# A graph-attention kernel: the fold of W1 as columns over two pairs of banks, and x, score rows, W1 and mask stores in other places

## The chip, the cores and the metric

The kernel runs on one core of a Trainium2 chip. The metric is device time in microseconds, of which a lower one is better, as the median of several executions. The core has five engines with a queue of instructions each: TensorE (PE), VectorE (DVE), ScalarE (ACT), GpSimd (POOL) and SyncE (SP); SyncE issues all transfers here.

## The reference

Two graph-attention layers over the same edges, with a residual and a layer norm.

```python
x, src, dst = ...                       # (1250, 768), 20000 edges, sorted by dst
src = concatenate([src, arange(1250)]); dst = concatenate([dst, arange(1250)])

def _gat_layer(x, src, dst, W, a_src, a_dst, bias, concat):
    h = (x @ W).reshape(N, H, C)
    al_s = einsum('nhc,hc->nh', h, a_src)
    al_d = einsum('nhc,hc->nh', h, a_dst)
    e = leaky_relu(al_s[src] + al_d[dst], 0.2)
    m = segment_max(e, dst)
    ex = exp(e - m[dst])
    alpha = ex / (segment_sum(ex, dst)[dst] + 1e-16)
    out = segment_sum(h[src] * alpha[:, :, None], dst)
    out = out.reshape(N, H * C) if concat else out.mean(axis=1)
    return out + bias

h   = elu(_gat_layer(x, src, dst, W1, att_src1, att_dst1, b1, concat=True))   # W1 768 x 2048, 4 heads of 512
out = _gat_layer(h, src, dst, W2, att_src2, att_dst2, b2, concat=False)       # W2 2048 x 768, 1 head
result = layernorm(x + out)
```

## The kernel before

Nodes are cut into ten blocks of 125 (B = 125, NB = 10). The edges become a dense count matrix C, and each layer is then a dense attention over blocks. The change touches only the first part of the program, up to the first attention chunk.

**Windows.** C is built in NW = 30 windows of 41 or 42 destination columns. For each window w VectorE makes seven one-hots (L1338, `ring`) from a table that ScalarE shifted (L987), TensorE multiplies them onto the slots' one-hots (`oh_lo`, L1714) between an opening product with zeros (L1706) and a closing one (L1717), and ScalarE copies the result into C (L993, "strip"). Window w uses bank w % 3 and waits until the window before the last but one has been copied. The `for w in range(NW)` loops of PE, ACT and DVE carry all other work of this part between windows, each at window numbers given by the constants XW, FS, CT, WSPL and WROW.

**The fold.** The attention vectors are multiplied into W1, so that the scores come straight from x. For each of 16 blocks of 128 columns of W1 (`fold_step`, L1637): six transposes of 128x128 into banks 3 and 4 (L1645), a copy to `wT` by ScalarE (L1018), and a product with the 8 columns of `acz` as weights and wT's 768 columns moving, into 8 rows of banks 5 and 7 (L1655). FS = 8 steps go ahead of window 0, two follow it, and one each window 1 to 7. Then ScalarE copies the 8x768 rows to `warow` (L1023, L1024), TensorE transposes them back to columns (L1766), and they are rounded to `wahi` and the rest `walo` (fp32r pairs: every exact product is three: hi x hi, hi x lo, lo x hi, L1683 to L1685).

**x.** From window XW - 1 = 10 on one block of x a window is transposed (L1674) in banks 6 and 7; ScalarE rounds it to the high part of `xa` (L963, L964), VectorE subtracts for the low part (L1308, L1310). SyncE stores both parts of each block to `xT_scratch` (L656), for heads 1 to 3. The raw x (`xall`) lies where W1's three tiles will be, so W1 can be loaded only when all of x has been transposed.

**Counts and masks.** From window CT = 8 on, every third window, the counts of one block are clipped (L1326), transposed into banks 3 to 5 (L1726), turned into a mask by ScalarE (L1001, L1003; two buffers, so mask b waits for the store of mask b - 2), stored by SyncE (L650), and later loaded back (L671) for the maxima on VectorE (L1364).

**Score rows** (L1738) are computed in windows 21, 22 and 23, a group of blocks each, when all of x is ready, into banks 6 and 7.

**W1 of head 0** is loaded (L644) behind the store of the tenth block, rounded by ScalarE after windows 26 to 28 (L968) and its rest made by GpSimd (L897). Then TensorE makes h in ten blocks (L1696), eight of them before the shift `gcol` is needed.

[...]

## Time and profile before

| | us |
|---|---|
| runs (three) | 952.14, 952.80, 955.18 |
| median | 952.8 |
| the profiled execution | 957.13 |
| its span, first to last instruction | 955.3 |
| TensorE busy | 887.2 (93%) |
| VectorE busy | 606.9 (64%) |
| ScalarE busy | 424.1 (44%) |
| GpSimd busy | 223.3 (23%) |
| mean granted TensorE clock | 0.977 |

The trace is one execution. Busy time is that of each engine's own instructions; a line L is one of the kernel before. TensorE's weight loads (PEld) run beside its products. A granted clock of 1.00 is full speed, 0.50 half.

### The profile page before, as it was taken

The numbers are of one execution on the slowest core, as the hardware profiler recorded it, in microseconds if no ns is written. First come the engines' busy times: TensorE is split into PE (matmuls) and PEld (weight loads), VectorE is DVE, ScalarE is ACT, GpSimd is POOL, SyncE is SP. The second block draws the span as 40 slices with busy tenths as digits, with TensorE's granted clock in tenths as the row PEclk, the third lists the DMA queues.
The fourth block names the chain that finished last, engine by engine and source line by source line (L and its number), as shares of the span: only waits on it lengthen the run. The fifth ranks groups of instructions, "written<-read, shape, count | busy, mean of one in ns | idle before, by whom it ended". The sixth has DMA issues, their size and how long they took to land.

```text
span 955.3 us, 15152 instructions
## 1 busy us (share of the span) xinstructions
PE 887.2 (93%) x5719; PEld 800.6 (84%) x5719; DVE 606.9 (64%) x1155; ACT 424.1 (44%) x686; POOL 223.3 (23%) x148
## 2 busy tenths in 40 slices
PE   4997885999999999999999998989999999699996
PEld 2455553889888998889988897989999999699996
DVE  9547743658893698828887388663222344397887
ACT  5346433257643675437663385852111111387300
POOL 1000003035321243122431266500000000154452
PEclk9999897999999999999999999999999999889999
DMA  8508994553467334582164333446232441400223
GB/s 299 134 1 119 151 169 134 137 151 132 158 193 189 121 115 139 170 202 95 38 193 117 103 132 121 135 142 150 54 84 47 78 75 30 98 3 2 59 88 97
DMA packets 64451, 111.19 MB, mean 116 GB/s; under 512 B 31772, under 2 KB 33464, under 8 KB 63004
## 3 DMA queue, kind: packets, MB, share of 16 engines
q1 hardware_dynamic: 64379, 110.22, 45.1%
q8 instruction: 46, 0.75, 0.4%
q14 instruction: 26, 0.21, 0.1%
HBM read 85.25 MB, written 24.94 MB: 115 GB/s over the span
## 4 chain that ended last, share of the span: by engine, by line
PE 65%; DVE 12%; issue 8%; POOL 6%; ACT 3%; SPq 3%; DMA 2%; DVEq 1%; POOLq 0%; ACTq 0%
PE ps L1683 19%; PE ps L1685 18%; PE ps L1684 18%; POOL pbuf L586 5%; PE ps L1714 3%; PE ps L1655 2%; DVE pbuf L599 2%; PE ps L1804 2%; SPq L656 2%; PE ps L1645 1%; DVE h2f L1594 1%; DMA w1raw<-in_L_gnn_W 1%; DVE h2f L1568 1%; DVE ring L1338 1%; DVE vbuf L1413 1%
## 5 line engine op out<-in xcount | busy, mean ns | idle before, releaser
L586 POOL TENSOR_TENSOR pbuf<-pbuf,grow 125x625 f32<-125x625 f32 x100 | 170.4, 1704 | 549.0 <-ACT pbuf L571 248.8
L1683 PE MATMUL ps<-hx,PThi 125*125 125x260 f32 (+5 forms) x800 | 228.2, 285 | 6.7 <-DVE vbuf L1407 3.8
L1685 PE MATMUL ps<-hx,PTlo 125*125 125x260 f32 (+5 forms) x800 | 225.9, 282 | 0.0
L1684 PE MATMUL ps<-hlo,PThi 125*125 125x260 f32 (+4 forms) x800 | 225.6, 282 | 0.0
L1683 PEld LDWEIGHTS ps<-hx,PThi 125*125 125x125 f32 x800 | 149.4, 187 | 11.3 <-DVE PTlo L613 3.5
L1684 PEld LDWEIGHTS ps<-hlo,PThi 125*125 125x125 f32 x800 | 149.8, 187 | 1.5
L1685 PEld LDWEIGHTS ps<-hx,PTlo 125*125 125x125 f32 x800 | 149.7, 187 | 0.0
L599 DVE SCALAR_TENSOR_TENSOR pbuf<-pbuf,counts 125x625 f32<-125x625 f32 x100 | 98.6, 986 | 25.3 <-ACT pbuf L593 25.1
L1683 PE MATMUL ps<-W2p,hT 128*125 128x384 f32 x320 | 109.7, 343 | 3.2 <-DVE hT L1419 1.7
L608 ACT ACTIVATE PThi<-pbuf 125x625 fp32r<-125x625 f32 x80 | 57.8, 723 | 114.4 <-DVE pbuf L599 57.5
L1685 PE MATMUL ps<-W2p,hT 128*125 128x384 f32 x320 | 108.1, 338 | 0.0
L1684 PE MATMUL ps<-W2p,hT 128*125 128x384 f32 x320 | 108.1, 338 | 0.0
L613 DVE TENSOR_TENSOR PTlo<-pbuf,PThi 125x625 fp32r<-125x625 f32 x80 | 79.3, 992 | 41.7 <-ACT PThi L608 41.5
L593 ACT ACTIVATE pbuf<-pbuf,s_sl 125x625 f32<-125x625 f32 x100 | 81.1, 811 | 45.6 <-POOL pbuf L586 45.4
L1419 DVE TENSOR_TENSOR hT<-ps,hT 128x500 fp32r<-128x500 f32 x40 | 25.2, 673 | 109.4 <-ACT hT L1105 109.4
L1338 DVE TENSOR_SCALAR ring<-table,ekey 125x420 bf16<-125x420 uint16 (+1 forms) x210 | 57.6, 348 | 44.1 <-PE ps L1717 14.4
L1683 PE MATMUL ps<-h2x,PT 125*125 125x384 f32 (+9 forms) x250 | 77.7, 311 | 4.7 <-DVE PT L613 4.2
L1105 ACT ACTIVATE hT<-ps 128x500 fp32r<-128x500 f32 x40 | 21.2, 586 | 133.9 <-PE ps L1804 133.9
L571 ACT ACTIVATE pbuf<-drow,s_up 125x625 f32<-125x625 f32 x100 | 80.3, 805 | 0.0
L1684 PE MATMUL ps<-h2lo,PT 125*125 125x384 f32 (+7 forms) x250 | 77.3, 309 | 0.0
L1685 PE MATMUL ps<-h2x,PT 125*125 125x384 f32 (+9 forms) x250 | 77.3, 309 | 0.0
L1685 PE MATMUL ps<-W1hi,xr 128*125 128x512 f32 x180 | 71.0, 395 | 0.0
(187 smaller groups left out, 1611.4 us busy)
## 6 DMA issues: line engine op xcount, KB each, us to landing
xr<-xT_scratch SPq DMA_DIRECT2D x30, 750.0 KB, 4.7
nbm<-mask_scratch SPq DMA_DIRECT2D x40, 273.4 KB
hidden_scratch<-vbuf SPq DMA_DIRECT2D x40, 224.0 KB
hblk<-hidden_scratch SPq DMA_DIRECT2D x10, 896.0 KB
xT_scratch<-xa SPq DMA_DIRECT2D x20, 375.0 KB, 11.5
w1f<-in_L_gnn_W SPq DMA_DIRECT2D x12, 512.0 KB, 9.3
w1raw<-in_L_gnn_W SPq DMA_DIRECT2D x4, 1536.0 KB, 7.9
w2raw<-in_L_gnn_W SPq DMA_DIRECT2D x14, 384.0 KB, 5.1
```

Source lines behind the costliest of these rows:

```text
L571: act.activation(pslot(c), src[:, g * GN:(g + 1) * GN], ACT.Relu, scale=UP, bias=bias).then_inc(z_done, 1)
L586: pool.tensor_tensor(pslot(c), pslot(c), src[:, g * GN:(g + 1) * GN], ALU.add).then_inc(e_done, 1)
L593: act.activation(pslot(c), pslot(c), ACT.Exp, scale=SLOPE, bias=bias).then_inc(p_done, 1)
L599: dve.scalar_tensor_tensor(pslot(c), pslot(c), 1.0, C[:, b, g * GN:(g + 1) * GN], ALU.min, ALU.mult).then_inc(pc_done, 1)
L608: act.activation(hi_slot(c), pslot(c), ACT.Copy).then_inc(pt_hi, 1)
L613: dve.tensor_tensor(lo_slot(c), pslot(c), hi_slot(c).bitcast(F32), ALU.subtract).then_inc(pt_lo, 1)
L1338: oh = dve.tensor_scalar(ring[:, w % 2, v, 0:win_cols(w)], table[:, w % TR, 0:win_cols(w)], ekey[:, bass.ds(at_slot(first, i, v), 1)], Non ...
L1419: lo = dve.tensor_tensor(ht_part(n % 2, 1, a), PS[:, bank, 0:4 * B], ht_part(n % 2, 0, a).bitcast(F32), ALU.subtract)
L1683: pe.matmul(dst, ahi, bhi, start=start, stop=False, skip_group_check=shared)
L1684: pe.matmul(dst[:, 0:n], ahi, blo, start=False, stop=False, skip_group_check=shared)
L1685: return pe.matmul(dst, alo, bhi, start=False, stop=stop, skip_group_check=shared)
L1714: t = pe.matmul(win_bank(w), oh_lo[:, bass.ds(at_slot(first, i, v), 1), :].rearrange("p o n -> p (o n)"), ring[:, w % 2, v, 0:win_cols(w)] ...
```

## The change

- **Fold:** wT becomes the weights (six products of 128x128 with 8 moving columns of `acz`), and the result comes as columns in bank 7. The row copy, its transposes and `warow` go. Transposes of step i use banks 3 and 4 or 5 and 6 in turn, and wait for the copy of step i - 2. Eleven steps stand ahead of window 0 in place of eight.
- **Windows:** banks 0, 1, 2 up to window 11, then banks 0 and 1 alone; bank 2 then holds the score rows.
- **x:** four windows sooner (first block after window 6).
- **Score rows:** the first two groups in thirds, windows 13 to 15 and 16 to 18, the last one at window 19; each group waits only for its own blocks of x. Their transposes go from window 24 to window 20.
- **Counts and masks:** one block, three windows, sooner.
- **W1 of head 0:** its load stands between the stores of x blocks 4 and 5, behind a wait for all ten blocks; rounded after windows 23 to 25, and the rest made by VectorE after windows 24 to 26, not by GpSimd.
- **SyncE:** the stores of x blocks 6 to 9 stand behind the score rows' store and load, among mask stores and loads. ScalarE waits for all stores of x before its first rounding of P.

```diff
-XW = 11
-FS = 8
+XW = 7
+FS = 11
 FU = 16
 FE = FU - FS
-CT = 8
-WSPL = 26
-WROW = 21
+CT = 5
+WSPL = 23
+WROW = 13
+WX = 12
...
+def bank_of(w):
+
+    return w % WRING if w < WX else w % 2
+
+
+def last_in_bank(w):
+
+    return max((v for v in range(w) if bank_of(v) == bank_of(w)), default=None)
...
+        def row_bank(c):
+
+            return PS[0:2 * H, WRING - 1, 0:(TCH[c][1] - TCH[c][0]) * B]
+
+        def row_steps(w):
+
+            u = w - WROW
+            if 0 <= u < 6:
+                return u // 3, range(2 * (u % 3), 2 * (u % 3) + 2)
+            return (2, range(KD)) if u == 6 else (None, ())
+
+        def fold_banks(i):
+
+            return PS[:, 3 + 2 * (i % 2):5 + 2 * (i % 2), 0:DH]
+
         def win_bank(w):
 
-            return PS[0:B, w % WRING, 0:win_cols(w)]
+            return PS[0:B, bank_of(w), 0:win_cols(w)]
...
-            store_nb(0)
-            for j in range(NB):
+            def store_xT(j):
                 sp.wait_ge(xt_lo, j + 1)
                 for u in range(2):
                     sp.dma_start(xT_d[j, :, u, :].rearrange("p (k n) -> p k n", k=KD), xa[:, u, :, j, :].bitcast(F32)).then_inc(xT_stored, 16)
-                if j % 3 == 0:
-                    store_nb(j // 3 + 1)
+
+            store_nb(0)
+            store_xT(0)
+            store_xT(1)
+            store_nb(1)
+            store_xT(2)
+            store_xT(3)
+            store_nb(2)
+            store_xT(4)
+            store_nb(3)
+            sp.wait_ge(xt_lo, NB)
             load_w1(0)
-            store_nb(5)
+            store_xT(5)
+            store_nb(4)
...
+            store_xT(6)
+            store_nb(5)
             for b in range(MR - 1):
                 load_nb(0, b)
+            store_xT(7)
             store_nb(6)
+            store_xT(8)
             store_nb(7)
+            store_xT(9)
+            store_nb(8)
             sp.wait_ge(strip_done, NW)
             load_drow(0, 0)
-            store_nb(NB - 2)
             store_nb(NB - 1)
...
-            for k in range(KD):
-                split_w1(0, k)
...
-                act.activation(wT[:, u % 2, :].rearrange("p (a k) -> p a k", a=2), PS[:, 3:5, 0:DH], ACT.Copy).then_inc(wt_sb, 1)
-
-            def folded_rows_out():
-
-                act.wait_ge(wrow_ps, 1)
-                act.activation(warow[:, 0:DH], PS[0:2 * H, 5, 0:DH], ACT.Copy)
-                act.activation(warow[:, DH:D], PS[0:2 * H, 7, 0:DH], ACT.Copy).then_inc(wrow_sb, 1)
+                act.activation(wT[:, u % 2, :].rearrange("p (a k) -> p a k", a=2), fold_banks(u), ACT.Copy).then_inc(wt_sb, 1)
...
                 if w == FE:
-                    folded_rows_out()
-                if w == FE + 1:
                     act.wait_ge(wcol_ps, 1)
...
+                if KD - 1 in row_steps(w)[1]:
+                    score_rows_out(row_steps(w)[0])
...
-                if j in (1, 2):
-                    mask_out(NB - 3 + j)
+                if j == 1:
+                    mask_out(NB - 1)
...
+            act.wait_ge(xT_stored, 32 * NB)
...
+                if w > WSPL and w <= WSPL + 3:
+                    split_w1(0, 2 * (w - WSPL) - 2)
+                    split_w1(0, 2 * (w - WSPL) - 1)
+                if w == FE + 1:
...
-                    if i >= 1:
-                        pe.wait_ge(wt_sb, i)
+                    if i == 1:
+                        pe.wait_ge(plan, 8)
+                    if i >= 2:
+                        pe.wait_ge(wt_sb, i - 1)
                     for k in range(KD):
-                        t = pe.transpose(PS[:, 3 + k // 3, k % 3 * 128:(k % 3 + 1) * 128],
+                        t = pe.transpose(fold_banks(i)[:, k // 3, k % 3 * 128:(k % 3 + 1) * 128],
                                          w1f[:, i // 4, k, i % 4 * 128:(i % 4 + 1) * 128], ident[:, :])
                     t.then_inc(wt_ps, 1)
...
-                    for a in range(2):
-                        t = pe.matmul(PS[0:2 * H, 5 + 2 * a, 0:DH], acz[:, u, :], wT[:, u % 2, a * DH:(a + 1) * DH],
-                                      start=u == 0, stop=u == FU - 1)
+                    for k in range(KD):
+                        t = pe.matmul(PS[:, 7, 2 * H * k:2 * H * (k + 1)], wT[:, u % 2, k * 128:(k + 1) * 128], acz[:, u, :],
+                                      start=u == 0 and k == 0, stop=u == FU - 1, skip_group_check=True)
                     if u == FU - 1:
-                        t.then_inc(wrow_ps, 1)
+                        t.then_inc(wcol_ps, 1)
...
-                    pe.wait_ge(strip_done, w - WRING + 1)
+                    pe.wait_ge(strip_done, last_in_bank(w) + 1)
...
-            def score_rows(c):
+            def score_rows(c, ks):
 
                 lo, hi = TCH[c]
-                if c == 0:
-                    pe.wait_ge(xt_lo, NB)
-                if c == 2:
-                    pe.wait_ge(rows_sb, 1)
-                for k in range(KD):
-                    t = products(PS[0:2 * H, 6 + c % 2, 0:(hi - lo) * B],
+                if ks[0] == 0:
+                    pe.wait_ge(xt_lo, hi)
+                    if c == 0:
+                        pe.wait_ge(strip_done, WX)
+                    else:
+                        pe.wait_ge(rows_sb, c)
+                for k in ks:
+                    t = products(row_bank(c),
                                  ((wahi[:, k, :], walo[:, k, :]), (xa[:, 0, k, lo:hi, :].rearrange("p b n -> p (b n)"),
                                    xa[:, 1, k, lo:hi, :].rearrange("p b n -> p (b n)"))),
                                  k == 0, k == KD - 1)
-                t.then_inc(rows_ps, 1)
+                if ks[-1] == KD - 1:
+                    t.then_inc(rows_ps, 1)
...
-                if w == FE:
-                    pe.wait_ge(wrow_sb, 1)
-                    for k in range(KD):
-                        t = pe.transpose(PS[:, 7, 2 * H * k:2 * H * (k + 1)], warow[:, k * 128:(k + 1) * 128], ident[0:2 * H, 0:2 * H])
-                    t.then_inc(wcol_ps, 1)
...
+                if row_steps(w)[1]:
+                    score_rows(*row_steps(w))
+                if w == WROW + 7:
...
-                if j < 2:
-                    transpose_counts(NB - 2 + j)
+                if j == 0:
+                    transpose_counts(NB - 1)
```

TensorE, ahead of window 0. Before, a fold step between two windows' worth of work; `w1f` is W1 as loaded, `ident` the identity, names read out<-moving,weights:

```order
25 L1645 MATMUL ps<-ident_50,w1f_80 128x128 [waits wt_sb]
26 L1645 MATMUL ps<-ident_50,w1f_80 128x128 x5
27 L1655 MATMUL ps<-wT_123,acz_122 8x384 [waits wt_sb]
28 L1655 MATMUL ps<-wT_123,acz_122 8x384
37 L530 TENSOR_LOAD rng_i_108 [waits lo_pad,lo_v,lo_made,consts_v,ranges]
38 L1706 MATMUL ps<-zcols_105,ident_b_51 125x420
```

And after:

```order
37 L1676 MATMUL ps<-ident_50,w1f_80 128x128 [waits wt_sb,ld_wf1]
38 L1676 MATMUL ps<-ident_50,w1f_80 128x128 x5
39 L1686 MATMUL ps<-acz_122,wT_123 128x8 [waits wt_sb]
40 L1686 MATMUL ps<-acz_122,wT_123 128x8 x5
49 L554 TENSOR_LOAD rng_i_108 [waits lo_pad,lo_v,lo_made,consts_v,ranges]
50 L1737 MATMUL ps<-zcols_105,ident_b_51 125x420
```

Two products with 384 moving columns have become six with 8, and the window's plan is fetched after 48 rows in place of 36.

SyncE, around the load of W1 of head 0, before:

```order
42 L656 DMA xT_scratch<-xa_81 128x6x125 [waits xt_lo]
43 L656 DMA xT_scratch<-xa_81 128x6x125
44 L650 DMA mask_scratch<-nbs0_87 112x1250 [waits nbs_done]
45 L650 DMA mask_scratch<-nbs0_87 13x1250
46 L644 DMA w1raw_75<-in_L0_gnn_W1 128x6x512
47 L650 DMA mask_scratch<-nbs1_83 112x1250 [waits nbs_done]
48 L650 DMA mask_scratch<-nbs1_83 13x1250
49 L728 DMA rows_scratch<-rows_82 8x1250 [waits rows_sb]
50 L700 DMA srow_98<-rows_scratch 112x1250 [waits rows_stored]
```

And after:

```order
32 L674 DMA mask_scratch<-nbs_83 112x1250 [waits nbs_done]
33 L674 DMA mask_scratch<-nbs_83 13x1250
34 L668 DMA w1raw<-in_L_gnn_W 128x6x512 [waits xt_lo]
35 L679 DMA xT_scratch<-xa 128x6x125 [waits xt_lo]
36 L679 DMA xT_scratch<-xa 128x6x125
37 L674 DMA mask_scratch<-nbs_87 112x1250 [waits nbs_done]
38 L674 DMA mask_scratch<-nbs_87 13x1250
39 L761 DMA rows_scratch<-rows 8x1250 [waits rows_sb]
40 L733 DMA srow<-rows_scratch 112x1250 [waits rows_stored]
42 L679 DMA xT_scratch<-xa 128x6x125 [waits xt_lo]
```

The load has twelve rows fewer ahead of it: the stores of five blocks of x and of one mask now stand behind it, four of those blocks behind the score rows as well.

## Rows read from the trace of the kernel before

**Rows 1.** The page's slices, 40 equal ones: granted clock and DMA, in tenths.

```profile
PEclk9999897999999999999999999999999999889999
DMA  8508994553467334582164333446232441400223
```

**Rows 2.** Chain of waits, 136 to 195 us: start, us, engine, line.

```profile
136.20 11.06 DMA w1raw<-in_L_gnn_W
...
151.78 4.29 DVE ring L1338 x5
156.21 1.62 PE ps L1714 x4
...
194.87 0.18 DVE gcol L623
```

**Rows 3.** Who waited for whom, 69 to 160 us: total, times, longest.

```profile
DVE ring L1338 <- ACT table L987: 10.6, 2, 9.1
...
ACT nbs L1001 <- DMA mask_scratch<-nbs: 6.3, 1, 6.3
```

**Rows 4.** Timeline of SyncE's queue, 79 to 190 us: start, us, instruction.

```profile
78.99 0.97 SPq L656 DMA_DIRECT2D xT_scratch<-xa  x2
...
165.57 5.56 SPq L650 DMA_DIRECT2D mask_scratch<-nbs  x4
...
173.52 15.82 SPq L671 DMA_DIRECT2D nbm<-mask_scratch  x16
```

**Rows 5.** Timeline of TensorE, 14 to 45 us: fold steps, windows 0 and 1.

```profile
14.31 1.54 PE L1645 MATMUL ps<-ident,w1f 128*128 128x128 f32 x6 [6.64 <-DMA w1f<-in_L_gnn_W]
...
20.33 0.88 PE L1645 MATMUL ps<-ident,w1f 128*128 128x128 f32 x6
...
22.53 0.88 PE L1645 MATMUL ps<-ident,w1f 128*128 128x128 f32 x6
...
33.49 0.39 PE L1706 MATMUL ps<-zcols,ident_b 125*125 125x420 bf16 x1
...
37.47 1.52 PE L1645 MATMUL ps<-ident,w1f 128*128 128x128 f32 x6
...
43.12 0.39 PE L1706 MATMUL ps<-zcols,ident_b 125*125 125x420 bf16 x1
...
44.62 0.85 PE L1645 MATMUL ps<-ident,w1f 128*128 128x128 f32 x6
```

**Rows 6.** The same, its instructions with 8 moving columns.

```profile
71.03 0.53 PE L1766 MATMUL ps<-ident,warow 8*128 8x8 f32 x6 [1.34 <-ACT warow L1024]
...
132.33 1.25 PE L1781 MATMUL ps<-ident,rows 8*125 8x8 f32 x10 [0.86 <-ACT rows L1029]
```

**Rows 7.** Timeline of ScalarE: a mask and a rounding of h [idle before].

```profile
143.52 1.00 ACT L1001 ACTIVATE nbs<-ps 125x1000 bf16<-125x1000 f32 x1 [6.32 <-DMA mask_scratch<-nbs]
...
194.18 0.60 ACT L972 ACTIVATE hx<-ps 125x512 fp32r<-125x512 f32 x1 [3.59 <-PE ps L1685]
```

**Rows 8.** Timeline of VectorE: the slots' one-hots.

```profile
10.15 18.94 DVE L1300 TENSOR_TENSOR oh_lo<-colid,elo 125x1000 bf16<-125x1000 uint16 x17
```

**Rows 9.** Timeline of TensorE: x, blocks 0 and 9, and the first score rows.

```profile
76.20 0.83 PE L1674 MATMUL ps<-ident,xall 125*128 125x125 f32 x6
...
109.25 0.86 PE L1674 MATMUL ps<-ident,xall 125*128 125x125 f32 x6
...
115.99 0.38 PE L1683 MATMUL ps<-xa,wahi 128*8 128x500 f32 x1
...
120.09 0.34 PE L1706 MATMUL ps<-zcols,ident_b 125*125 125x420 bf16 x1
```

**Rows 10.** Stretches: each engine's busy time, granted clock, DMA share, GB/s.

```profile
13.00:15.00 2.00, 0.69 (x3) 0.69 (x4) 2.00 (x3) 1.14 (x2) 0.00 (x0) 1.00 1.05 387
37.00:38.00 1.00, 1.00 (x6) 0.83 (x5) 1.00 (x6) 0.33 (x1) 0.00 (x0) 0.50 0.08 17
```

**Rows 11.** W1lo on VectorE: ns min/median/max, first and last start.

```profile
L1319 DVE TENSOR_TENSOR W1lo<-w1raw,W1hi x18: 677/684/2050, 220.1 to 465.9; 128x512 fp32r<-128x512 f32 x18
```

More of the change, by code:

```diff
@@ L261, in gat_kernel @@
         wT = sb("wT", [128, 2, D], F32)
-        warow = sb("warow", [2 * H, D], F32)
+        cursor[0] += 4 * D
         ehi = sb("ehi", [B, SLOTS], F32)
@@ L1029, in score_rows_out @@
                 act.activation(rows[:, TCH[c][0] * B:TCH[c][1] * B],
-                               PS[0:2 * H, 6 + c % 2, 0:(TCH[c][1] - TCH[c][0]) * B], ACT.Copy).then_inc(rows_sb, 1)
+                               row_bank(c), ACT.Copy).then_inc(rows_sb, 1)
             act.wait_ge(consts, 8)
```

14 lines of the change are left out of this document (2 added, 12 removed).

## The prediction

> **What bounds the kernel now.** I read the page first. TensorE is busy for 93% of the span, but its granted clock dips to 7 tenths in slice 6 (143 to 167 us; a slice is 23.9), where TensorE stood idle, and the DMA row is at 8 and 9 tenths in the three slices before, 72 to 143 us [rows 1]. All lines that the diff touches run before 200 us. So I next read the chain of waits there [rows 2]. Up to 136 us the chain lies in SyncE's queue, in the stores of the transposed x (L656, 2 to 4 us each to issue), then 11.06 us in the load of W1 for head 0 (L644), which was issued at 136.20 behind all twenty of those stores, then in ScalarE's rounding of W1, then in one-hots that VectorE makes at 0.86 us apiece (4.29 for five) while GpSimd works beside it, and only at 156.21 does TensorE get the second half of its last window, which ends at 157.8. The waits say what stood [rows 3]: ScalarE waited 6.3 us at a mask for an older mask to leave its buffer, then for W1, and VectorE waited 9.1 us for ScalarE's table. Window 29 and the first block of h are late by this.
>
> Behind it come eight blocks of h on TensorE, and on VectorE the maxima over masks that SyncE must first have stored and loaded back. The last mask pair is issued at about 171 (the end of the 5.56 us row of L650), the loads run from 173.52 to 189.3, and the shift gcol is ready at 195.05 [rows 2, 4]. TensorE's eighth block ends at about 194.2, where ScalarE begins to round it [rows 7]. From there on the program is the same in both kernels, and its order too, so I forecast the time at which gcol is ready and carry the difference to the end.
>
> **The fold.** A fold step is now six transposes (0.88, of which 0.07 lie over the next instruction, so 0.81) and two products of 384 columns, four instructions, since a float32 product is two. The steps are 2.20 us apart, 20.33 to 22.53 [rows 5], so the products take 1.39. After, the six transposes stay, and the product becomes six with wT (128x128) as weights and 8 columns that move: twelve instructions. None such is in the trace. Nearest below: six instructions with 128-wide float32 weights and 8 moving columns (L1766) take 0.53 us, of which the last one's own 0.20 is pipeline, so 0.066 each, and twelve are 0.79. Nearest above: ten with 125-wide weights and 8 columns (L1781) take 1.25, so 0.11 each, and twelve are 1.3 [rows 6]. I take 0.066, since that row has the width of the new weights; the reserve is that it is a transpose and not a product. A step is then s = 0.81 + 0.78 = 1.59 us. ScalarE's copy, also 0.81, hides beside it, since the second pair of banks lets the next transposes run during the copy; with one pair the chain would be transposes, copy, product.
>
> The Trainium skill speaks against this choice (TensorE: Matmul & The Clock Gate, LDWEIGHTS and Weight-path perf modes): the time of a weight load goes with its columns, 128 columns over 1.2 GHz or 107 ns, and the fast load is not given to float32. By that rule twelve would be about 1.3 us. The trace disagrees with it at L1766, with 0.066 us for 128 float32 columns; this stays open for products, and the sum by the rule is that of the second case below.
>
> Ahead of window 0 stand eleven steps in place of eight. They begin at 14.31, the first transposes at the slow 1.54 [rows 5], and end at 14.3 + 1.5 + 11 x 1.59 = 33.3. VectorE's one-hots of the slots are done at 29.1 [rows 8], so window 0 begins as before (33.49), with three steps more done. Then window 0 (4.0, from 33.49 to 37.47) and windows 1 to 6 at 1.50 (43.12 to 44.62) [rows 5] carry five steps in place of eight. The old way back, copying the folded rows, transposing them into columns (1.34 idle and 0.53 of TensorE at 71.03, [rows 6]) and 0.84 us of ScalarE, is gone. With one transpose of counts (0.7) and 2 us for the plan fetches, VectorE's own pace and the wait for walo, the first block of x is transposed at 14.3 + 1.5 + 15.5 s + 4.0 + 9.0 + 0.7 + 2 = 31.5 + 15.5 s = 56.1, against 76.20 [rows 9]. That is 20 us earlier, 9.3 of it by the shorter step, the rest by beginning four windows sooner and by three steps that stand ahead of window 0 in the slack of the one-hots.
>
> **x and its stores.** Ten blocks ran from 76.20 to 109.25, 3.67 us each [rows 9]. Nothing in a block's circle (transpose, two copies on ScalarE, two subtractions on VectorE, between seven one-hots) changes, so the tenth is ready at about 93. In windows 13 to 15 TensorE also has 1.36 us of score rows (six of 0.228, as eighteen filled 115.99 to 120.09, [rows 9]) and passes VectorE's pace by about 0.7 each; I let that stand in the rounding. Store 0 goes at about 59.5, against 78.99 [rows 4].
>
> **The DMA queue** is what this earlier start buys, so I sum it. Twenty stores of 375 KB and four mask pairs of 305 KB went from 78.99 until the mask buffer was free at 143.5 [rows 4, 7]: 8.93 MB in 64.5 us, 138 GB/s. After, twenty stores and ten mask pairs, 10.8 MB, take 78 us at that rate. To these come W1 (1.57 MB, 4 us at the 387 GB/s that the same matrix reached at the start, [rows 10]) and some 10 us for the score rows, with their wait for landing, srow, two mask loads and half of drow. From 59.5 this ends at 152, where the last mask has landed, against 173.5. The maxima behind it took 21.5 us to gcol, so 173.5. I add 2 us for mask copies 7 to 9, each of which waits on ScalarE for the mask two before it, and these stores now sit behind x blocks 6 to 9 (mask 9 is wanted at about 137 and mask 7 has left at about 139). Queued behind such a wait are the table, the strip and the rounding of h, and TensorE behind these. So **gcol at 175.5**, 19.5 earlier.
>
> **TensorE must not be later.** W1 is issued when block 9 is done, at 93, past stores 5 to 9 and masks 4 and 5; it lands at about 104 even with the 11 us of before. It is wanted at window 23. Windows 16 to 22 with the score rows come to 95 + 3 x 2.9 + 3.5 + 3.2 + 2 x 2.4 = 115, so 10 us of cover; without that cover each us late is one us on the windows. The low parts of W1 move from GpSimd (1.28 each, six in 7.5 us, beside VectorE's slow one-hots of [rows 2]) to VectorE, which does the same for later heads in 0.68, so 4.1 us of VectorE's path in windows 24 to 26 [rows 11]. Windows 21 to 29 at 2.4 and these 4.1 end at about 131, against 157.8. Eight blocks of h of 4.19 us (3.59 of wait and 0.60 of ScalarE, [rows 7]) and one transpose of counts end at 167, 8 us ahead of gcol. The ring of two banks from window 12 asks for the copy of the window before the last, 0.5 us of ScalarE that is done while the window between runs; I cost it at nothing, hidden by that window's 1.5 us, and at up to 1.3 us a mask if ScalarE stands at a mask copy. SyncE's last x store is issued near 137, long before ScalarE's new wait for it ahead of its first rounding of P.
>
> **The sum.** The profiled execution took 957.13 with a span of 955.3. Less 19.5 it is 937.6. The median of the three runs is 952.8, 4.3 lower, and less 19.5 it is 933.3. My forecast is **933.5**, its own range 928 to 939.
>
> **Rivals.** *The new products load their weights at 0.11.* Then s = 2.1, the first block of x comes 8 us later, everything on the queue with it: 941.5. For it: the 125-wide rows and the skill's rule; against: the 128-wide row.
>
> *The clock stays low through the fold.* The first transposes at 14.31 and 16.75 took 1.54 for six, and only after the long products of 18.2 to 20.3 had streamed did six take 0.88 [rows 5]; at 37 to 40, after a gap, the granted clock was 0.50 [rows 10], the 1.2 GHz level, and a fold step took 3.5. The new fold has no long products. At the low level the transposes are 1.28 and twelve loads 1.0 to 1.5, so s is 2.3 to 2.8 until a window or two have streamed, and by 31.5 + 15.5 s the first block comes at 67 to 75: 944 to 952. The Trainium skill (TensorE: Matmul & The Clock Gate, PE-mode transpose) says that transposes don't count as busy for the clock in the usual way, which would favour this case; that the transposes at 20.33 ran at the upper level right behind the long products neither bears it out nor contradicts it, as no row has transposes alone for long.
>
> *Slower than before.* The same place, but a load of 128 float32 columns in a product costs at the low clock what a transpose costs there, 0.21 us: then a product is 2.6, s is 3.8 for the eleven steps ahead of window 0, and as much for the five behind if the windows between don't lift the clock. The forecast turns at s = 2.9, where the first block is no earlier than 76.2. With s at 3.8 for eleven steps and 2.9 for the others the first block comes at 86, 10 us late: 962.
>
> *The queue is not the bound.* If the stores run faster with their cover of other traffic gone, TensorE's 167 binds, gcol is at 168: 926.
>
> **Chances.** The forecast 0.50; slow loads 0.15; low clock in the fold 0.20, of which a quarter lies within 0.3% of before (about what a measurement of this kernel can tell from no change); slower 0.08; the queue not the bound 0.07. So faster 0.87, same 0.05, slower 0.08. The range 928 to 951 leaves out the last case, the slower one and the end of the low clock.
>
> **What would show it.** In the profile after: twelve products of a fold step in about 0.8 us and steps 1.6 apart; the first x transpose at 56; the W1 load issued at about 93 and its rounding without a wait; no GpSimd work before 170; stores of x from 59 to about 145 with the DMA engines full; gcol at 175 and the stretch behind it unchanged. The forecast fails if fold steps stay over 2 us, if the masks block ScalarE for more than a few us, or if the stores' rate of 138 GB/s is not that of the queue but of the blocks that feed it.

## The result and the profile after

The change does not give 19 us; depending on where it is measured it costs or gives less than 1%. Twelve runs of the changed kernel took 952.91 to 971.7 us, median 960.12, beside twelve of the kernel before at 951.7 to 955.6, median 953.87. The ratio is 1.0053, 95% interval [1.0028, 1.0077]. On a second chip, where the kernel before took 960.29, ten runs gave 949.36 to 968.47, median 957.63, ratio 0.9949 [0.9924, 0.9974]. The ratios, here and below, leave a version's longest runs out (of the changed kernel three of twelve and two of ten), and the spread is itself a finding: 19 us, where the kernel before keeps within 4. The profiled execution here took 971.7, span 969.9, so a second one (span 960.1, on the second chip) is used beside it.

The timeline of TensorE in the changed kernel, 23 to 97 us, is to be read beside [rows 5] and [rows 9] (columns: start, us, engine, line, operation, names, shapes, count):

```profile
23.24 1.52 PE L1676 MATMUL ps<-ident,w1f 128*128 128x128 f32 x6
24.55 2.57 PE L1686 MATMUL ps<-acz,wT 128*128 128x8 f32 x12
26.97 1.52 PE L1676 MATMUL ps<-ident,w1f 128*128 128x128 f32 x6
...
53.11 0.59 PE L1737 MATMUL ps<-zcols,ident_b 125*125 125x420 bf16 x1
...
65.39 0.59 PE L1737 MATMUL ps<-zcols,ident_b 125*125 125x420 bf16 x1
65.77 2.66 PE L1745 MATMUL ps<-ring,oh_lo 125*125 125x420 bf16 x7
...
94.77 1.41 PE L1745 MATMUL ps<-ring,oh_lo 125*125 125x420 bf16 x7
...
96.05 0.84 PE L1705 MATMUL ps<-ident,xall 125*128 125x125 f32 x6
```

A fold step is 26.97 - 23.24 = 3.73 us, 1.31 for the six transposes and 2.42 for the twelve instructions of the product, 0.20 each. The forecast had 1.59, and the old step was 2.20. The transposes are those of [rows 5] and take 1.52 where they took 0.88, and seven products of a window take 2.66, at 94.77 only 1.41. So TensorE ran at the lower of its two levels, 1.2 GHz, from the first step to 94 us. The granted clock does not say so: it reads 1.00 for all of this stretch (in order: the stretch and its length in us, busy us and number of instructions of PE, PEld, DVE, ACT and POOL, granted clock, DMA share, GB/s).

```profile
14.00:94.00 80.00, 77.92 (x346) 71.80 (x347) 28.14 (x64) 18.82 (x29) 0.00 (x0) 1.00 0.30 86
```

SyncE's queue and ScalarE's roundings of h are to be read beside [rows 4] and [rows 7]. First SyncE:

```profile
133.28 0.39 SPq L668 DMA_DIRECT2D w1raw<-in_L_gnn_W  x1
...
178.93 0.75 SPq L674 DMA_DIRECT2D mask_scratch<-nbs  x2
```

The seven products of the last window, on TensorE's timeline:

```profile
170.66 1.42 PE L1745 MATMUL ps<-ring,oh_lo 125*125 125x410 bf16 x7
```

ScalarE's timeline, the first rounding of W1 and the roundings of h before and behind gcol:

```profile
154.92 1.15 ACT L1003 ACTIVATE W1hi<-w1raw 128x512 fp32r<-128x512 f32 x2
...
202.71 0.60 ACT L1007 ACTIVATE hx<-ps 125x512 fp32r<-125x512 f32 x1 [3.54 <-PE ps L1716]
206.89 0.60 ACT L1007 ACTIVATE hx<-ps 125x512 fp32r<-125x512 f32 x1 [3.59 <-PE ps L1716]
```

VectorE's timeline, the last maximum and the shift:

```profile
205.59 1.46 DVE L1395 CUSTOM_DVE_ANT_0 junk<-nbm,srow 125x1250 bf16<-125x1250 bf16 x1
...
207.58 0.17 DVE L647 SCALAR_TENSOR_TENSOR gcol<-negm,al 125x10 f32<-125x10 f32 x1
```

The first block of x comes at 96.05 (before 76.20), W1 is rounded without a wait, the last window ends at 172.1 (before 157.9), and gcol starts at 207.58 (before 194.87, [rows 2]). So gcol is 12.7 later and the span 14.6; the stretch behind gcol, forecast as unchanged, took 762.3 us against 760.4 (760.5 in the second profile). From the first block of x to gcol it was 118.7 us before and is 111.5 now: behind the fold the change does win, 7 us.

### The profile page after: what moved, and what is told of

The parts are those of the page before. It is cut to its first block, busy times and chain, and to the rows that moved or that the text cites. A ratio compares the mean times of both kernels' runs of the same rounds, so it can differ in the third digit from the quotient of the medians.

```text
span 969.9 us, 15398 instructions
## 1 busy us (share of the span) xinstructions
PE 914.7 (94%) x5841; PEld 847.1 (87%) x5841; DVE 606.7 (63%) x1161; ACT 423.7 (44%) x684; POOL 215.1 (22%) x142
## 4 chain that ended last, share of the span: by engine, by line
PE 69%; DVE 11%; issue 8%; POOL 6%; ACT 3%; DMA 1%; DVEq 1%; SPq 0%; POOLq 0%; ACTq 0%
PE ps L1714 19%; PE ps L1716 18%; PE ps L1715 18%; POOL pbuf L610 5%; PE ps L1745 4%; PE ps L1686 4%; PE ps L1676 2%; DVE pbuf L623 2%; PE ps L1833 2%; DVE h2f L1623 1%; DVE h2f L1597 1%; DMA w1f<-in_L_gnn_W 1%; DVE vbuf L1442 1%; DVE bnst L1614 1%; DVE vbuf L1435 1%
## 5 line engine op out<-in xcount | busy, mean ns | idle before, releaser
L1366 DVE TENSOR_SCALAR ring<-table,ekey 125x420 bf16<-125x420 uint16 (+1 forms) x210 | 53.0, 325 | 55.8 <-PE ps L1737 24.8
```

Source lines behind the costliest of these rows:

```text
L1366: oh = dve.tensor_scalar(ring[:, w % 2, v, 0:win_cols(w)], table[:, w % TR, 0:win_cols(w)], ekey[:, bass.ds(at_slot(first, i, v), 1)], Non ...
```

## The experiments

Theory C says that the loss is TensorE's level: the new fold's loads and 8-column products neither lift it to the upper one nor hold it there, so steps and windows up to 94 us run at half speed. Against it stand S (the new order of queue and windows loses the time) and W (the price of the weight loads is what costs, at whatever level). Further rivals are named with the run that they bear on.

Each version took its median beside the kernel before on the same chip; only ratios go from one chip to another (the chip of after_again, e5, e6 and e7 is the one with 960.29 for the kernel before; the others had 953.0 to 954.2). The table is read from each profiled execution, in us: where the first block of x is transposed, where the last window ends, where gcol starts.

| version | first x | last window ends | gcol | span |
|---|---|---|---|---|
| before | 76.2 | 157.9 | 194.9 | 955.3 |
| changed | 96.0 | 172.1 | 207.6 | 969.9 |
| after_again | 87.4 | 164.2 | 199.6 | 960.1 |
| e1, old fold | 69.6 | 148.4 | 183.8 | 944.3 |
| e2, new fold only | 84.7 | 163.3 | 200.7 | 963.0 |
| e3, stream ahead | 80.4 | 159.3 | 194.7 | 955.1 |
| e4, streams in the fold | 90.9 | 170.2 | 205.7 | 965.4 |
| e5, W1 last | 69.8 | 165.9 | 201.3 | 961.8 |
| e6, W1lo on GpSimd | 70.9 | 152.7 | 188.2 | 948.7 |
| e7, x late | 78.8 | 143.5 | 195.2 | 957.2 |
| e8, stream and old fold | 70.6 | 147.8 | 183.2 | 943.2 |
| e9, both products | 92.1 | 168.1 | 203.6 | 965.6 |
| e10, 13 steps ahead | 67.7 | 151.2 | 186.7 | 949.0 |
| e11, one long product | 75.9 | 155.0 | 190.4 | 950.9 |

In all eleven profiles with the change's early x (all but before, e2 and e7) gcol starts 35.4 to 35.5 us behind the end of the last window; in before it is 37.0 and in e2 37.4.

**e1: the change with the old fold.** One pair of banks, two products of 384 columns, rows copied and transposed back; all else as changed.

```diff
-                    for k in range(KD):
-                        t = pe.matmul(PS[:, 7, 2 * H * k:2 * H * (k + 1)], wT[:, u % 2, k * 128:(k + 1) * 128], acz[:, u, :],
-                                      start=u == 0 and k == 0, stop=u == FU - 1, skip_group_check=True)
+                    for a in range(2):
+                        t = pe.matmul(PS[0:2 * H, 5 + 2 * a, 0:DH], acz[:, u, :], wT[:, u % 2, a * DH:(a + 1) * DH],
+                                      start=u == 0, stop=u == FU - 1)
```

> The changed kernel with the fold of the kernel before: two products of 384 moving columns, rows as result, one pair of banks, the rows copied and transposed back; all other moves of the change stay (eleven steps ahead of window 0, x four windows sooner, score rows in pieces, W1 between stores). Theory C (the clock: the new products don't lift TensorE's clock, and the whole fold runs at 1.2 GHz): the old products lift it at about 20 us, a step takes 2.2, window 0 begins at 14.3 + 1.5 + 11 x 2.2 = 40, and the first block of x is transposed at about 68 in place of 96 in the changed kernel and 76 before; then the other moves give what they have, 5 to 10 us under before, so 944 to 949. Rival S (the schedule costs: masks and stores of x behind the score rows, two banks for windows): no faster than before, 952 or more, with ScalarE waiting at masks.

Measured: 946.43 (945.0 to 947.18, four runs), ratio 0.9919 [0.9901, 0.9937], faster than both kernels. TensorE's timeline of e1:

```profile
21.85 1.46 PE L1694 MATMUL ps<-wT,acz 128*8 128x384 f32 x4
23.24 0.87 PE L1684 MATMUL ps<-ident,w1f 128*128 128x128 f32 x6
24.05 1.46 PE L1694 MATMUL ps<-wT,acz 128*8 128x384 f32 x4
25.43 0.87 PE L1684 MATMUL ps<-ident,w1f 128*128 128x128 f32 x6
...
40.77 0.39 PE L1745 MATMUL ps<-zcols,ident_b 125*125 125x420 bf16 x1
...
69.56 0.86 PE L1713 MATMUL ps<-ident,xall 125*128 125x125 f32 x6 [1.10 <-DVE walo L1395]
```

Steps of 2.19 and windows at the upper level from 22 us on. Against the changed kernel, the eleven steps ahead of window 0 are 12.3 us shorter (40.77 against 53.11), windows 0 to 4 with five steps 15.6 (22.0 against 37.6), and the stretch from window 5 to the first block of x is 1.4 longer, since e1 has the old way back of the rows there: 26.5 us to the first block of x, and 23.8 at gcol. So the change without its fold is faster than before, rival S falls, and the loss is all in the fold.

**e2: the kernel before with the new fold only** (columns as result, two pairs of banks; nothing moved, so the diff is the fold's part of the change).

> The kernel before with the new fold alone: six products of 128x128 with 8 moving columns, result as columns, two pairs of banks; eight steps ahead of window 0 as before, nothing else moved. Theory C: the clock is low from the first transpose on, a step takes 3.7 in place of 2.2, sixteen steps and the windows between them come 25 to 30 us later, the first block of x at about 102, and the whole is 20 to 28 us slower, 975 to 980; in executions where the clock rises sooner less. Rival S: within 5 us of before.

Measured: 964.85 (956.3 to 977.41, ten runs), ratio 1.0085 [1.005, 1.0119]. Its TensorE goes through both levels, which gives the price at each:

```profile
50.30 1.52 PE L1641 MATMUL ps<-ident,w1f 128*128 128x128 f32 x6
51.61 2.57 PE L1651 MATMUL ps<-acz,wT 128*128 128x8 f32 x12
54.03 0.59 PE L1702 MATMUL ps<-zcols,ident_b 125*125 125x420 bf16 x1
54.41 2.62 PE L1710 MATMUL ps<-ring,oh_lo 125*125 125x420 bf16 x7
...
56.90 0.85 PE L1641 MATMUL ps<-ident,w1f 128*128 128x128 f32 x6
57.58 1.41 PE L1651 MATMUL ps<-acz,wT 128*128 128x8 f32 x12
58.84 0.37 PE L1702 MATMUL ps<-zcols,ident_b 125*125 125x410 bf16 x1
```

From one start to the next, twelve instructions take 54.03 - 51.61 = 2.42 at the lower level, 0.20 each, and 58.84 - 57.58 = 1.26 at the upper one, 0.105 each (1.34, or 0.11, in e9 below). The old product was 1.38. So even at the upper level the new step is 0.68 + 1.26 = 1.94, or 2.05 by e9, against 2.19: 0.14 to 0.25 us shorter and not 0.6. The fold's loss is at the lower level, as theory C has it, and the gain that never was lies in the price, as W has it. One half of theory C is not borne out: once up, at 57 us, the level stayed up until 79 us, through seven new products and the windows between them, so the new fold can run at the upper level once it is there.

**e3: a stream ahead of the fold.** Fifteen zero products of 420 columns while TensorE waits for the first part of W1:

```diff
+            for i in range(15):
+                pe.matmul(PS[0:B, 2, 0:WM], ident_b[0:B, 0:B], zcols[:, 0:WM], start=True, stop=True, skip_group_check=True)
             for i in range(FS):
                 fold_step(i)
```

> The changed kernel with fifteen products of 420 bfloat16 columns (of zeros, into a bank that nothing uses yet) ahead of the fold, in the 6.6 us in which TensorE waits for W1. Theory C: they lift the clock before 14.4, so the fold begins at 2.4 GHz: transposes 0.8, twelve instructions of the product 1.2 if a load there costs half of the 0.2 it cost in the changed kernel, steps of 2.0; if the clock then stays up, window 0 begins at 36 and the first x at 62, and the kernel takes about 940; if light steps let it fall again, it falls within the fold and the time lies between 940 and 960. Theory W (a load of 128 float32 columns for a product costs 0.2 us at either clock): transposes 0.8 but products still 2.4, steps of 3.1, first x at 80, 948 to 952.

Measured: 954.77 (949.58 to 959.16), ratio 1.0003 [0.998, 1.0026]. The durations say that the stream lifted the level for a moment: its fifteen products took 4.61 us, against 5.51 for the same fifteen in e8 below:

```profile
7.74 4.61 PE L1699 MATMUL ps<-zcols,ident_b 125*125 125x420 bf16 x15
14.30 2.48 PE L1676 MATMUL ps<-ident,w1f 128*128 128x128 f32 x12 [1.95 <-DMA w1f<-in_L_gnn_W]
```

Then TensorE stood idle for 1.95 us, and from about 15 us the fold ran at the lower level; the column reads 0.50 until 58 us. Here it does record what the durations say (steps of 3.73 again). The stretches of e3:

```profile
8.00:14.00 6.00, 4.35 (x15) 2.62 (x14) 5.79 (x16) 5.93 (x16) 0.00 (x0) 1.00 1.05 396
15.00:24.00 9.00, 9.00 (x45) 8.91 (x44) 9.00 (x9) 2.43 (x3) 0.00 (x0) 0.50 1.05 361
24.00:58.00 34.00, 32.34 (x152) 31.05 (x151) 8.86 (x19) 7.26 (x10) 0.00 (x0) 0.50 0.38 94
```

**e4: e3 with three more such products in each step ahead of window 0.**

> As the run with fifteen products ahead of the fold, and three more such products (420 bfloat16 columns of zeros) behind each of the fold steps that stand ahead of window 0. Theory C: the clock rises before the fold and cannot fall in it; a step ahead of window 0 takes 2.0 + 0.55 = 2.55, window 0 begins at 42 and the five later steps take 2.0: the first x at 66, about 943 to 946, and less spread between executions than the changed kernel has. If the run without these three keeps its clock, this one is 5 us slower than it. Theory W: steps of 3.6, slower than the run with fifteen alone.

Measured: 956.62 over ten runs from 943.67 to 978.6, ratio 0.9963 [0.9931, 0.9995]; with a spread of 35 us this settles nothing as to time. In the profiled execution (967.19) the granted clock was 0.50 through the fold, steps of 4.78, first x at 90.9. One run, at 943.67, beat e1. The mean granted clocks of the ten runs go with their times, from 0.983 for that one to 0.945 for the two longest, so the level came up early in some executions and not in others, of one and the same program. Three 420-column products in every step did not bring it up in the profiled one. They are bfloat16 and all zeros; whether length, type or values make the difference to the old fold's products was not run.

**after_again: the changed kernel once more.**

> The changed kernel itself, once more, for a second profiled execution. Its twelve times spread over 953 to 972 us, where the kernel before and the kernel with the old fold keep within 4 us. Theory C (the clock): steps and windows run at half the clock from the start until it rises, and when it rises differs between executions; so in a second profile the steps are again 3.7 us where the clock is low, the products 2.4 to 2.6 us for twelve and 1.4 where it is high, and the span moves with the place of the first x transpose: 969.9 - 96.05 = 873.8 us lie between the two in the first profile, and 874 +- 3 in this one. Rival S (the schedule: queue and buffers lose the time, wherever the clock stands): the first x transpose is again at 96 and the spread sits behind it.

Measured: the result above. First x at 87.4, and 960.1 - 87.4 = 872.7 us behind it, where the first profile had 873.9: the difference between the two profiled executions of one kernel, which are from two chips, lies nearly all ahead of the first x. TensorE's level rose at 75.6 us, 19 us earlier. Its timeline in after_again:

```profile
70.41 2.57 PE L1686 MATMUL ps<-acz,wT 128*128 128x8 f32 x12
...
75.64 0.85 PE L1676 MATMUL ps<-ident,w1f 128*128 128x128 f32 x6
76.33 1.40 PE L1686 MATMUL ps<-acz,wT 128*128 128x8 f32 x12
```

**e9: both products.** In the steps ahead of window 0 the two long products of the old fold stand behind the twelve new ones, and nothing reads them.

```diff
+                    if i < FS:
+                        for a in range(2):
+                            pe.matmul(PS[0:2 * H, 2, 0:DH], acz[:, u, :], wT[:, u % 2, a * DH:(a + 1) * DH],
+                                      start=True, stop=True, skip_group_check=True)
```

> The changed kernel, and in each step ahead of window 0 the two 384-column products of the old fold on top of the twelve of 8 columns (their result goes into a window's bank and isn't used). This is only more work for TensorE: 1.39 us a step at the upper level, 2.73 at the lower. Theory C (the clock stays low because nothing in the new step is long enough in columns, and falls to the price of its loads alone): the clock rises within the first three or four steps, as with the old fold; steps are 0.81 + 1.40 + 1.39 = 3.6 us against 3.73 without the additional work, windows and steps behind run at full clock, 3.5 us a pair instead of 6.5, first x at 73 to 78 instead of 87 to 96, and the whole takes 948 to 954 us with a spread of under 5 us: more work, less time. Rival W (the twelve loads are what holds the engine at the lower pace, whatever stands beside them): steps of 3.73 + 2.7 = 6.4 us, first x behind 110, over 980 us.

Measured: 961.42 (951.35 to 973.8), ratio 1.0024 [0.9991, 1.0058]. The time and the spread missed the expectation, and the profile, of an execution of 967.37, shows why. TensorE's timeline of e9, the first long products, steps with them, window 0 and then a step without them:

```profile
16.98 2.62 PE L1686 MATMUL ps<-acz,wT 128*128 128x8 f32 x12
19.53 2.73 PE L1692 MATMUL ps<-wT,acz 128*8 128x384 f32 x4
22.19 0.93 PE L1676 MATMUL ps<-ident,w1f 128*128 128x128 f32 x6
...
31.16 1.46 PE L1692 MATMUL ps<-wT,acz 128*8 128x384 f32 x4
32.55 0.87 PE L1676 MATMUL ps<-ident,w1f 128*128 128x128 f32 x6
33.26 1.40 PE L1686 MATMUL ps<-acz,wT 128*128 128x8 f32 x12
34.59 1.46 PE L1692 MATMUL ps<-wT,acz 128*8 128x384 f32 x4
...
55.19 2.01 PE L1749 MATMUL ps<-ring,oh_lo 125*125 125x420 bf16 x7 [1.66 <-DVE ring L1366]
...
57.07 1.52 PE L1676 MATMUL ps<-ident,w1f 128*128 128x128 f32 x6
58.38 2.57 PE L1686 MATMUL ps<-acz,wT 128*128 128x8 f32 x12
```

Steps of 3.43 at the upper level from 22 to 53 us, shorter than the changed kernel's 3.73 in spite of 1.38 us of additional work. The level fell inside window 0, behind 1.66 us in which TensorE stood idle; behind that window, where the long products are left out, the steps are 3.73 again, until 87 us. The twelve loads run at either pace (so W falls as a cause of the lower level). The level came up with the first long products, and once lost it did not come back for 31 us without them; that leaving them out is what makes it fall is not shown.

**e11: one long product in all steps but the last.**

```diff
+                    else:
+                        pe.matmul(PS[0:2 * H, 7, 128:512], acz[:, u, :], wT[:, u % 2, 0:DH],
+                                  start=False, stop=False, skip_group_check=True)
```

> The changed kernel, and in all sixteen steps but the last one 384-column product beside the twelve of 8 columns (its result stands in columns that nothing reads): 0.69 us more a step at the upper level, about 1.3 at the lower. With two such products in the eleven steps ahead of window 0 the steps ran at the upper level from the third on, and fell back to 3.73 us in the five steps behind, where they were left out. Theory C (the share of the step that streams long columns decides): with one in every step the upper level is reached early and kept through windows 0 to 6; steps of 0.81 + 1.40 + 0.69 = 2.9 us, first x at 76 to 80, 950 to 956 us within 5 us of each other, where the changed kernel itself spreads over 19 us. Rival F (one is too little: the clock falls whenever the twelve loads run, as behind window 0 in the kernel with both products): steps of 5.0 us wherever it is down, first x at 95 to 110, 968 to 985 us; in between, a first x between 80 and 95 with a spread as the changed kernel's says that it is caught late and by chance.

Measured: four runs of 952.74, 961.64, 965.36 and 979.28, ratio 1.0105 [1.0071, 1.0139]. The profiled one is the 952.74. TensorE's timeline of e11:

```profile
16.98 1.60 PE L1686 MATMUL ps<-acz,wT 128*128 128x8 f32 x12
18.52 0.81 PE L1691 MATMUL ps<-wT,acz 128*8 128x384 f32 x2
```

Steps of 2.79 at the upper level from 18 to 44 us, a drop in the steps behind window 0 (twelve in 2.57 at 49.25), up again at 54.5, first x at 75.9. These numbers are those of theory C, but the first rise is not its doing: the first twelve new products already took 1.60 in place of 2.62, ahead of the first long product. So the level can also come up early without a long product before it. The spread isn't theory C's either. What would bring the level up early in every run, beside the new products, stays open. With the old fold the times keep within 2.2 us in e1 and e8 (four runs each) and within 5.5 in e5, e7 and e10 (nine or ten runs).

**e8: e1 with the stream of e3 ahead of it.**

> The change with the old fold, and ahead of its first step the same fifteen zero products of 420 bf16 columns as in the kernel with the stream before the fold (about 6 us of work in time in which TensorE waits for the first part of W_fc). Theory C (the 384-column products of the old fold lift the clock and keep it, the 8-column ones let it fall): the granted clock may be down at the first step, but is up by the third or fourth as without the stream, the steps are 2.19 us, the first x transpose comes at 66 to 70 and the whole takes 943 to 948 us. Rival D (the stream itself is what makes the clock fall, whatever the fold's products are): it reads 0.50 through the fold, steps of 4.3 us or more, first x behind 80, 955 to 965 us.

Measured: 946.0 (944.95 to 946.44), ratio 0.993 [0.9913, 0.9947], as e1. TensorE's timeline of e8:

```profile
7.64 5.51 PE L1707 MATMUL ps<-zcols,ident_b 125*125 125x420 bf16 x15
15.17 0.87 PE L1684 MATMUL ps<-ident,w1f 128*128 128x128 f32 x6 [2.02 <-DMA w1f<-in_L_gnn_W]
16.94 1.54 PE L1684 MATMUL ps<-ident,w1f 128*128 128x128 f32 x6 [0.90 <-ACT wT L1055]
18.41 2.22 PE L1694 MATMUL ps<-wT,acz 128*8 128x384 f32 x4
20.56 0.88 PE L1684 MATMUL ps<-ident,w1f 128*128 128x128 f32 x6
```

What rival D forecast did not come: the steps are 2.19 from 20.6 us. But the level fell here too, between the first transposes (0.87) and the second (1.54), as it did in e3 at 15 us. What differs is the way back: with the long products it was up again within 4 us, in e3 not before 58. The same holds around window 0, where the level is lost in e8, in e7 and in the kernel before as well: there it is back within 4 us, with the next old steps ([rows 5], 37.47 and 44.62). The stream gains nothing.

**e5, e6, e7: what the rest of the change gives.** All three are e1 with one part undone. e5 moves the load of W1 behind mask 6:

```diff
-            sp.wait_ge(xt_lo, NB)
-            load_w1(0)
             store_xT(5)
...
             store_nb(6)
+            load_w1(0)
             store_xT(8)
             store_nb(7)
```

> The change with the old fold, and the load of W1 back behind nearly all copies of x and masks (behind mask 6) on SP's queue. In the version with the old fold (946.4 us) it was issued at 108.0, between copies; here about 133. Theory X (nearly all of the 7 to 8 us that this schedule gains over the kernel before comes from x starting four groups earlier): ScalarE rounds W1 at window 23, near 125 us, and would wait for the load till about 143, so this costs even so: windows behind it are delayed, 951 to 957 us. Rival Q (the queue of DMAs is what ends last, and W1's 2.4 MB only change places in it): within 2 us of 946.4.

Measured: 963.55 (961.4 to 964.79), ratio 1.0029 [1.0014, 1.0044], 13.7 us more than e6 on the same chip; against e1 the two ratios make 10.6. From the list of who waited for whom in e5 (total, times, longest):

```profile
ACT W1hi L1004 <- DMA w1raw<-in_L_gnn_W: 18.1, 1, 18.1
```

W1, issued at 133.25, lands at 148.15. ScalarE stands for 18 us with the window copies queued behind it, and gcol is 13.1 later than in e6. Theory X has the mechanism, and its 951 to 957, given for e1's chip, holds: 1.0029 of that chip's 954.17 is 956.9. The load took 15 us among the stores where I had 10. (W1 of one head is 1.57 MB, not the 2.4 of rival Q.)

e6 gives the low parts of W1 back to GpSimd.

> The change with the old fold, and the low parts of W1 on GpSimd again (six of about 1.25 us each in the kernel before) where the change has VectorE do them in six of 0.6 to 0.7 us between windows. Theory (off the path): GpSimd is idle there, and the h blocks wait for the last window anyway: 946.4 within 1.5 us. Rival P (VectorE and GpSimd slow each other, or the six parts end late): GpSimd needs 7.5 us from the last rounding, the h blocks start up to 3 us later, 948 to 950 us.

Measured: 949.9 (948.61 to 950.45), ratio 0.9895 [0.9873, 0.9917]; e1 had 0.9919 [0.9901, 0.9937]. The intervals overlap, so no difference can be told.

e7 puts x, masks, score rows and the steps at the windows of the kernel before (XW 11, FS 8, CT 8, WSPL 26, WROW 21, WX 20).

> The change with the old fold, and with x, the folded steps, the masks and the score rows at the windows where the kernel before has them (x from window 11, eight steps ahead of window 0, masks from window 8, score rows from 21); what stays of the change is the order of SP's queue with W1 between copies, the low parts of W1 on VectorE and the score rows in pieces. Theory X: the first x transpose comes at 76 to 77 us instead of 67, and what hangs on it moves by as much: 953 to 956 us, as the kernel before. Rival Q (queue order gives most of the gain): 946 to 949 us.

Measured: 959.55 (956.68 to 961.41), ratio 0.9995 [0.998, 1.0011]: all of e1's gain is gone. Theory X gave the time, but the way is another. The last window ends at 143.5, 14.4 earlier than in the kernel before (W1 is there in time), and then ScalarE waits for mask buffers whose stores stand in SyncE's queue behind those of x. From the list of waits, 120 to 196 us:

```profile
ACT nbs L1038 <- DMA mask_scratch<-nbs: 22.7, 3, 8.9
```

gcol comes 51.7 us behind the last window in place of 35.4 in e1. So here the queue binds, and in e1, with x four windows earlier, it doesn't. The two moves are worth something only together: W1 between the copies frees the windows, the earlier x frees the masks.

**e10: e1 pushed further**, thirteen steps ahead of window 0 and x from window 5 (FS 13, XW 5, WROW 11, WX 10).

> The change with the old fold, pushed further: thirteen steps of the fold ahead of window 0 instead of eleven, x from window 5 instead of 7, score rows from window 11 instead of 13. Theory X (the time follows the place of the first x transpose one for one, as from the version of before's windows to the change's): first x at 64 to 66 instead of 69.6, 940 to 943.5 us on a chip where the version with eleven takes 946.4, ratio to before 0.986 to 0.988. Rival E (windows, masks and their loads end last by themselves from here on, and DMAs of x collide with more of them): first x moves as well, but the whole stays within 1.5 us of 946.4, ratio 0.990 to 0.993.

Measured: 951.02 (948.5 to 953.98), ratio 0.9976 [0.9959, 0.9993], worse than e1, outside both expectations. x came only 1.9 us earlier, and from there to the last window it was 83.5 us where e1 had 78.8. Its waits, 67 to 105 us, have more of some kinds than e1's 69 to 104, ScalarE for windows 16.7 against 12.4 and VectorE for walo 4.0 against 1.7, and two windows run at the lower level, at 69.3 and 83.4 (2.45 for seven), where e1 has one, at 82.6. Which of these costs the 5 us against e8, on the same chip, wasn't separated.

The best version is therefore e1 (946.43; e8 with 946.0 is not told from it): the change's schedule with the old fold.

## Why the prediction was wrong

**The step that failed is the length of a fold step**, s = 0.81 + 0.78 = 1.59 us. It measured 1.31 + 2.42 = 3.73. Two terms were wrong in it. One is the price of the new product, 0.066 us an instruction, twelve in 0.78: at the upper level it is 0.105 to 0.11, and a step 1.94 to 2.05. The other, and the larger, is the level, taken as the upper one throughout: at the lower one the product costs 0.20 an instruction and the transposes 1.31, and this is the rest, 1.7 to 1.8 us a step. For the price I had two rows in [rows 6], L1766 at 0.066 and L1781 at 0.11, and took the one with the same width of weights. Both are transposes (their moving side is the identity), with weights on 8 partitions, so neither had the kind of the new product. That the other row, L1781, came out right may be luck; no run here tells why the two rows differ. The page named in the prediction (the Trainium skill, TensorE: Matmul & The Clock Gate, LDWEIGHTS and Weight-path perf modes), with 107 ns for 128 columns, gives what e2 measured at the upper level, 0.105, and not my row's 0.066. The 0.20 at the lower level is not what that figure gives.

**The rival that came true** is the one with 0.08: 0.21 us a load at the lower level, s = 3.8, turning at 2.9. Measured were 2.42 for twelve and s = 3.73. It was too mild in one point. I let windows lift the clock behind window 0, but five windows of 2.60 to 2.66 us with steps between did not, in this execution. With s = 3.73 the prediction's own formula, 31.5 + 15.5 s, gives 89.3. Window 0 took 4.8 in place of 4.0 and windows 1 to 5 took 2.9 in place of 1.5, together 7.8, which makes 97.1; 96.05 was measured. So the sum to the first block of x held; its s and the pace of its windows did not, both by the level.

**Why the clock stayed low.** The evidence against the forecast stood in [rows 5]: the transposes were slow until the long products had streamed, and the change removes these. I gave it 0.28 in two rivals. With two long products in a step (before, e1, e5 to e10) the upper level is there from the third or fourth step in every profile. Without them it came at 57, 59, 69, 75 and 94 us in the profiles of e2, e3, e4, after_again and the changed kernel, and e9 against the changed kernel shows it with nothing else changed. With one, in e11, it came at 17 us, ahead of that product. So the long products bring the level up reliably; that the new steps let it fall is not shown, and what brings it up without them, at such different times, stays open. The rule cited with that rival (same page of the Trainium skill, PE-mode transpose: transposes are not counted as busy in the usual way) is not tested by these runs, since the twelve products, which are no transposes, stood beside the transposes at the lower level.

**The DMA queue as the bound is refuted for the changed order.** In the changed kernel the last mask pair went at 178.93, but from the third block on ScalarE's roundings of h wait 3.5 to 3.6 us each for TensorE, up to 206.89, and gcol starts 35.4 to 35.5 behind the last window in all eleven profiles. TensorE binds: my own path for it, 75 us from first x to last window and 36 for the blocks, measured 76.05 and 35.5. The 75 is in part luck. By the terms that the prediction gives (115 at the end of window 22, seven windows of 2.4 and 4.1 for the low parts) the last window ends at 136 and not at 131, so 80 us from the first x, and TensorE's path at 172, 3.5 us ahead of the forecast gcol and not 8. The rival "queue not the bound" had the mechanism right, with 0.07. Only in e7 do the stores bind.

**What held.** W1 was there in time, as forecast (issued when block 9 was done, rounding with no wait), and e5 shows what it was worth: 13 us at gcol. VectorE's low parts, forecast at 4.1 us in windows, cost no time that e6 can tell. The masks behind ScalarE, for which I added 2 us, cost nothing. The second pair of banks: the old step of 2.19 is 0.81 of transposes and 1.38 of products with no gap, so its copy was hidden with one pair already. The new order without its fold gave 7.7 us on the median (e1) and 11.1 at gcol, against 19.5 predicted for both together. Its first block of x came at 69.6 in place of the forecast 56.1, since the old step is 0.6 us longer than the forecast one and the old way back of the rows remains.

## What to carry to other kernels

Swapping the operands of a product so that few columns move under wide weights pays a weight load for each 128 columns; compare it with the streams that it replaces at both levels of the clock, and if what ran just before the level rose is what the change removes, work the sum out at the lower level too. When the nearest rows for a new instruction disagree, and none is of its kind, carry both prices through the sum and let the forecast stand only if both ends agree in sign. A load placed in a full queue is worth what stands behind its consumer: here the load of W1, issued 24 us later than in e6, cost 13.7.

## What the runs showed of the hardware

The granted clock read 1.00 for 80 us in which identical instructions took nearly twice their time (six transposes 1.52 and 0.85, seven window products 2.66 and 1.41), and 0.50 for the same durations in e3. In the profiles read here it reads 1.00 until the level has once been up and has fallen again: in e9 it reads 1.00 for the slow steps of 14 to 22 us, and 0.50 for steps of the same durations from 58 us on:

```profile
58.00:87.00 29.00, 29.00 (x122) 25.28 (x121) 7.52 (x29) 7.41 (x12) 0.00 (x0) 0.50 0.00 1
```

So in a profile's first stretch the durations tell the level and that column may not. In the first 80 us of the changed kernel's fold TensorE was busy for 77.92 and yet stayed at the lower level, and in e3 and e8 a level that had been up was down again by 17 us. The same program came up at 94 us in one profile and at 75 in another, on another chip. On one chip its twelve runs spread over 19 us, and e4's ten over 35; that this is the time of the rise fits the granted clocks of e4, and is argued for the changed kernel.
